# A two-layer graph network on one core: how many of each chunk's eight source columns TensorE looks up and how many POOL gathers

## The reference, cut to what matters

```python
def _L1_gnn_ref(x, edge_index, edge_attr, W1, b1, W2, b2, We1, be1, We2, be2, res_w, dot_scale, ln_g, ln_b):
    src, dst = (edge_index[0], edge_index[1])
    n = x.shape[0]
    for l in range(W1.shape[0]):
        h = _leaky(x @ W1[l] + b1[l]) @ W2[l] + b2[l]
        e = _leaky(edge_attr @ We1[l] + be1[l]) @ We2[l] + be2[l]
        msg = h[src] * e * dot_scale[l]
        agg = jax.ops.segment_sum(msg, dst, num_segments=n)
        out = x + agg * res_w[l]
        mu = jnp.mean(out, axis=-1, keepdims=True)
        var = jnp.mean(jnp.square(out - mu), axis=-1, keepdims=True)
        x = (out - mu) * jax.lax.rsqrt(var + LN_EPS) * ln_g[l] + ln_b[l]
    return x
```

## Time and profile before

| | us |
|---|---|
| median of 3 timed runs | 6974.49 |
| profiled execution, its own time | 6960.44 |
| its span, first to last instruction | 6958.6 |
| TensorE matmul busy | 5066.8 |
| DVE busy | 5088.1 |
| ACT busy | 4002.8 |
| POOL busy | 5252.7 |
| gathers of the five layers (2652), busy | 2574.6 |
| pause memsets in the whole kernel (3009), busy | 1077.1 |

### The profile page before, as it was taken

The page is one execution under the profiler, slowest core; times in us unless marked ns, Lnnn a source line. Parts: engine busy times, 40 slices in busy tenths (PEclk is TensorE's granted clock), DMA queues, the critical chain, the costliest instruction groups (busy, mean ns, idle before and its releaser), DMA issues.

```text
span 6958.6 us, 134654 instructions
## 1 busy us (share of the span) xinstructions
PE 5066.8 (73%) x48820; PEld 4673.8 (67%) x48820; DVE 5088.1 (73%) x12225; ACT 4002.8 (58%) x6886; POOL 5252.7 (75%) x7260
## 2 busy tenths in 40 slices
PE   7888833333333588887788887888878888788886
PEld 7777732222222488887788886888868888688886
DVE  8776666666666577777687776777767777677776
ACT  5666626555555256665466664666646666466664
POOL 6777777777777377777677776777767777677777
PEclk9999965555555699998899997999979999799998
DMA  4444427777777333333233332333323333233332
GB/s 110 109 108 109 108 64 242 242 242 239 238 240 239 118 90 94 97 99 87 75 95 94 100 96 65 98 98 97 93 68 96 96 97 96 65 96 97 96 97 75
DMA packets 509379, 828.59 MB, mean 119 GB/s; under 512 B 112942, under 2 KB 220069, under 8 KB 495662
## 3 DMA queue, kind: packets, MB, share of 16 engines
q1 hardware_dynamic: 373374, 650.98, 27.9%
q0 software_dynamic: 135344, 169.01, 13.5%
HBM read 385.16 MB, written 434.48 MB: 118 GB/s over the span
## 4 chain that ended last, share of the span: by engine, by line
POOL 26%; DVE 15%; issue 12%; PE 8%; DMA 3%; another core or an unknown queue 2%; ACT 1%; DVEq 0%; POOLq 0%; ACTq 0%
POOL gring L708 20%; PE psum L1368 6%; DVE arena L1769 6%; POOL rest L699 6%; DMA gring<-tableh,src_i 2%; DVE by_lane L1832 2%; DVE psum L1815 2%; DVE gring L1809 1%; DVE es_w L1769 1%; POOL agg L715 1%; DVE psum L1821 1%; PE psum L1382 0%; ACT gring L1006 0%; ACT gring L1010 0%
## 5 line engine op out<-in xcount | busy, mean ns | idle before, releaser
L708 POOL DMA_INDIRECT gring<-tableh,src_i x2652 | 2574.6, 971 | 921.3 <-issue 612.5
L1368 PE MATMUL psum<-penalty,arena 125*128 125x192 bf16 x24736 | 2418.7, 253 | 363.5 <-DVE gring L1769 150.6
L1368 PEld LDWEIGHTS psum<-penalty,arena 125*128 125x128 bf16 x24736 | 2149.2, 101 | 453.2 <-ACTq L1014 226.0
L1769 DVE TENSOR_SCALAR arena<-dst_f,node_id 125x640 bf16<-125x640 f16 x4556 | 1779.8, 437 | 0.1
L708 POOL DMA_INDIRECT gring<-table,src_i x1364 | 1384.1, 1015 | 441.0 <-issue 316.3
L699 POOL MEMSET rest<- 128x256 f32 x3009 | 1077.1, 358 | 200.8 <-DMA tableh<-arena 85.1
L981 ACT COPY psum<-diag 128x512 f32<-128x512 f32 x505 | 297.6, 590 | 1496.2 <-DVE psum L1815 856.4
L1815 DVE TENSOR_TENSOR psum<-psum,gring 128x512 f32<-128x512 f32 x505 | 349.5, 692 | 511.4 <-DMA gring<-tableh,src_i 395.3
L1145 PE MATMUL psum<-ident,by_lane 128*128 128x128 f32 x202 | 66.7, 434 | 878.4 <-DMA by_lane<-attr_last 772.1
L1382 PE MATMUL psum<-arena 128*128 128x128 f32 x4040 | 579.9, 287 | 165.5 <-issue 155.9
L1809 DVE TENSOR_REDUCE gring<-psum 128x128 f32<-128x384 f32 x505 | 352.1, 697 | 432.3 <-PE psum L1368 261.2
(11 more groups left out here) (272 smaller groups left out, 8095.3 us busy)
## 6 DMA issues: line engine op xcount, KB each, us to landing
rows<-arena SPq DMA_DIRECT2D x101, 1296.0 KB
acts<-arena SPq DMA_DIRECT2D x505, 256.0 KB
arena<-acts SPq DMA_DIRECT2D x505, 256.0 KB
rowsg<-run SPq DMA_DIRECT2D x505, 256.0 KB
gring<-tableh,src_i POOLq DMA_INDIRECT x2652
dst_f<-pe_src SPq DMA_DIRECT2D x430, 93.8 KB
rows<-run SPq DMA_DIRECT2D x101, 256.0 KB
gring<-table,src_i POOLq DMA_INDIRECT x1364
```

What stands on the lines that cost most here:

```text
L708: pool.indirect_dma_start(ring[:, s, k, :], None, table, bass.IndirectOffsetOnAxis(ap=src_i[:, c * K + k:c * K + k + 1], axis=0))\
L1368: ins = mm(found(n)[:, m, :], hot_at(n // 2, j)[:, at:at + P], parts[:, j, :, :].rearrange("q a f -> q (a f)"), start=(j == 0), stop=(j == ...
L1769: ins = ts(hot_at(pair, j), src_row[b], node_id[:, j:j + 1], None, ALU.is_equal)
```

## The change

KPE becomes (3, 3, 3, 3), so TensorE looks up three columns in every chunk and POOL gathers five. Both widths of one-hot tiles become 768, so the even pairs need 25 slices of that width: 17 in `arena`, 4 in `xin`, 2 in the integer tile of the destinations (`dst_i`), one in a new tile, one in `gring`; the odd pairs get 17 in `arena`, 4 in `es_w`, 4 in `gring`. To make room, `src_cols` becomes a view of `run1` and `rest` a view of `diag`, and POOL waits once, before its first gather, for `bc_ready`.

```diff
-KPE = (2, 3, 3, 3)
+KPE = (3, 3, 3, 3)
...
-NJA = 20
+NJA = 17
...
-        src_cols = sb("src_cols", [P, PE_COLS])
...
-        rest = sb("rest", [P, 256])
...
+        src_cols = run1[:, 0, :, :].rearrange("p k f -> p (k f)")[:, 0:PE_COLS]
...
+        hot_more = sb("hot_more", [NQ, WIDE[0] // 2])
         hot = ([], [])
         for b, tile, lo, hi in ((0, arena[0:NQ, :], 0, HOT // 2),
                                 (0, xin[:, :, :].rearrange("q j f -> q (j f)"), 0, NJ * F),
+                                (0, dst_i[0:NQ, :].bitcast(F32), 0, T), (0, hot_more[:, :], 0, WIDE[0] // 2),
                                 (1, arena[0:NQ, :], HOT // 2, HOT),
                                 (1, es_w[0:NQ, :, :].rearrange("p t h -> p (t h)"), L * CW, T * H),
-                                (1, gring[0:NQ, :], SL * K * F, SL * K * W2R)):
+                                (1, gring[0:NQ, :], SL * K * F, SL * K * F + 4 * WIDE[1] // 2),
+                                (0, gring[0:NQ, :], SL * K * F + 4 * WIDE[1] // 2, SL * K * W2R)):
...
+        rest = diag[:, :, :].rearrange("p a n -> p (a n)")
...
             issued, rests = [0], [0]
+            pool.wait_ge(bc_ready, 1)
...
-                    pool.memset(rest[:, :], 0.0).then_inc(rested, 1)
+                    pool.memset(rest, 0.0).then_inc(rested, 1)
```

More of the change, by code:

```diff
@@ L1460, in _ @@
             dve.wait_ge(edges_in, 128)
-            st.done(nc.vector.tensor_copy(src_cols[:, :].rearrange("p (c m) -> p c m", m=KMAX),
+            st.done(nc.vector.tensor_copy(src_cols.rearrange("p (c m) -> p c m", m=KMAX),
                                           src_i[:, :].rearrange("p (c k) -> p c k", k=K)[:, :, K - KMAX:]))
             dve.wait_ge(dve_steps, st.n)
-            ts(src_cols[:, :], src_cols[:, :], float(MID), None, ALU.subtract).then_inc(src_cols_set, 1)
+            ts(src_cols, src_cols, float(MID), None, ALU.subtract).then_inc(src_cols_set, 1)
             st.then(nc.vector.tensor_copy(dst_f[:, :], dst_i[:, :]))
```

## The result

The first comparison, four runs of each kernel in one session, gave 6886.17 us (6876.32 to 6895.57) for the changed kernel and 6977.53 for the kernel before: ratio 0.9869 [0.985, 0.9889], 91 us faster. The forecast was 6790, its range 6765 to 6865. Two later comparisons gave more: 0.9773 [0.9756, 0.9789] on chip 11 (6747.05 against 6905.4) and 0.9791 [0.9777, 0.9804] on chip 9 (6825.75 against 6971.89). The record doesn't name the chip of the first. So there are two questions: why 146 to 158 us and not 184 where things went well, and what took another 55 us or more in the first comparison.

The account below looks back on a forecast made before the run. POOL's gather stream was taken to bound the layers: 6960.4 us less 200.3 for 127 fewer gathers, plus 17 given back, made 6777; 14 for timed runs over the profiled one made 6791, about 6790. Range 6765 to 6865.

Parts of the forecast that it names:

- slow starts: TensorE's layer lookups at the lower clock after a gap, 8.54 us instead of 6.18; expected fewer, from 55 us a layer.
- hand-over: TensorE and DVE passing pairs of chunks in the layers: cycle at most 14.2 us, under POOL's 15.77; cost none.
- 7.10 us a chunk: TensorE's three-column chunk in the layers: lookup 6.18 plus products 0.92 us, 90% of POOL's 7.89.
- rival 1: TensorE takes over the bound in the layers through slow starts and "issue" gaps; put at 6890 us, chance 0.09.
- 17 us given back: Layers: POOL's gathers and memsets lengthen in proportion to DVE's share, 85/78, costing 0.09 * 188 = 17 us.
- POOL's excess: Mean over fastest time of POOL's layer instructions: 31 ns a gather, 58 ns a pause memset.
- bounds of -17 and 188 us: Range for the change in POOL's excess: shrinking by as much as 17 us, or at the outside doubling, 188 more.
- 98 us of wider one-hots: DVE's extra time for even pairs' one-hots, 640 to 768 wide; all would come back if blocking POOL, about 6872 us.
- POOL's stream as the layer's length: POOL's gathers and pauses, 1.577 us a gather, set each layer's time: near 796 us after the change.
- my own mark for "wrong" of 390: Sign against the forecast: POOL's pause memsets in the layers taking over 390 ns.
- nothing at the start: Kernel start: POOL's new wait for bc_ready costs zero, with 3 us of cover before the first gather at 40.44.
- Rivals 2, 3 and 4: In order: TensorE's idle time is structural, 7261 us, 0.05; collisions cancel the gain, 6962, 0.04; pauses set POOL's pace, 0.02.

Follow-up runs that it names:

- d: The changed kernel with POOL gathering three instead of five a chunk, two columns keeping old values; 6394.1 us, ratio 0.9157 to the kernel before.
- n_again: The changed kernel measured once more on chip 11, nothing else changed; 6747.05 us, ratio 0.9773 to the kernel before.
- r_third: The changed kernel measured once more on chip 9, nothing else changed; 6825.75 us, ratio 0.9791 to the kernel before.
- e: The kernel before, narrow one-hots kept, with five gathers in every chunk (one column of every fourth chunk stale); 6812.85 us, ratio 0.9758.
- a: The changed kernel with TensorE looking up and DVE reducing only two columns in every fourth chunk, POOL still gathering five; 6828.7 us, ratio 0.9773.
- b: The changed kernel with POOL gathering six and DVE reducing two columns in every fourth chunk, TensorE still looking up three; 7029.3 us, ratio 1.0066.
- h_rest1: The changed kernel with one pause memset after every fourth gather instead of three; 8093.9 us, ratio 1.1586 to the kernel before.
- j_quarter_rows: The changed kernel with the layers' gathers fetching 32 rows instead of 128; 7080.3 us, ratio 1.0158 to the kernel before.
- m_gat_burst2: The changed kernel with one pause memset after every second gather, only in the first block's attention pass; 6742.1 us, ratio 0.9672.

## Why the prediction was wrong

**What failed: "So I expect fewer slow starts, a granted clock of about 0.97 in the layers, and no bound", and with it the cost "none" of the hand-over.** The clock rose (0.99). But in the first comparison TensorE was the bound: DVE's waits for gathers fell to 0.8 us and the waits before the node gathers grew by 74 us over the five layers, a term that stood at nothing. Where I counted 7.10 us a chunk I took one undisturbed lookup for the mean. That is TensorE's pace with three gathers a chunk (7.11 in d), not beside five: "issue" gaps inside its lookups and its products of e were 320 us.

I had met these gaps in the rows of before, 107.2 + 155.9 us, and set them aside with "they lie mostly where its work isn't ready". For most of them that was right: in the trace of before, over all tiles, 195 us of them stand before the first product of a lookup or of an e, where waits are written, and 103 inside. The change took away nearly all of the first kind (7 us were left) and tripled the second. A gap inside one column's 25 products can't be a wait for data, and I didn't look for those. Yet their size in before doesn't foretell their size after it: on chip 9 they went from 89 to 51 us, and there the step held, as it did in n_again: POOL was the bound and the backlog gone.

It is rival 1, which had 0.09, but not by its sum: the slow starts that it counted were gone. Its price of 6890, beside a measured 6886, had no working behind it and came so close by luck.

**What was mis-sized: "17 us given back".** POOL's excess does not follow DVE's share. The price went from 1.579 to 1.601 on one chip, 2525 * 0.022 = 56 us. Put into the forecast's own sum, 6960.4 - 200.3 + 56 + 14 = 6830, against 6826 of r_third. The bounds of -17 and 188 us held it. In the first comparison it was as much, 2525 * 0.023 = 58. The Trainium skill, in SBUF — State Buffer (SBUF: two separate sides), has VectorE's two-port instructions and GpSimd block each other in turns. The prediction read it so that all 98 us of wider one-hots would come back, which the page does not say. The traces agree in kind: with wider one-hots beside them POOL's gathers go from 973 to 984 ns and its memsets from 377 to 383 (e and a), though ACT's were wider too. In size it was 38 to 50 us (a against e, b against the kernel before), about half of the 98 or less.

**What held.** 2525 gathers; POOL's stream as the layer's length where TensorE keeps up (806 us in r_third, forecast 796); no waits of POOL for line 1819 worth naming (6.9 us in 6); memsets at 378 ns in the first comparison, but 392 in r_third, over my own mark for "wrong" of 390; nothing at the start (first gather at 40.6 us, before 40.44). DVE and ACT stayed hidden. Rivals 2, 3 and 4 are out.

**What stays open.** Why the same program starves TensorE in one session and not in another. Each chip on record but one was used in one session only, and the chip of the first comparison isn't on record, so chip and session can't be told apart. Nor is it known what slows TensorE's supply: T says when the gaps come, not through what. Both regimes idle TensorE by about the same amount; an engine that waits for data now and then has time to be refilled, one that never waits has none. That would make it tip over, but I have not shown it.

## What to carry to other kernels

Before calling an engine "not the bound" by its busy time, look at its gaps inside one accumulation group (the products that add up in one place): "issue" gaps there are real and belong into its pace, though they can grow or shrink with the change. Where GpSimd's gathers run beside a dense straight-line stream of small matmuls, the gathers' rhythm is part of TensorE's speed: try half as many wider matmuls and other pause lengths before moving work over. And measure once more, in another session and on another chip, when two engines are within a few per cent of each other, since a gain of 1.3% in one session was 2.1 and 2.3% in two others with the same program.

## What the runs showed of the hardware

- The pauses cost POOL (717.6 + 72.9) / 2525 = 0.31 us a gather and pay for themselves: with one memset after four gathers instead of three, a layer takes 1013 to 1050 us (h_rest1), and 813 to 821 with three in a_pe_old on the same chip.
- A gather of 32 rows takes 914 ns of POOL (j_quarter_rows), one of 128 rows 977 in m_gat_burst2 beside it: nearly all of it is there whatever the rows.
- TensorE at 5840 products in 500 us held a granted clock of 1.00 in that stretch (d_three_gathers), at 3593 in 500 us with many gaps 0.82 (h_rest1).
